# Local attention of a two-layer transformer block: queries and keys held by token and then transposed

## What is computed

```python
h = shift_token(x)
q, k, v = jnp.split(h @ wqkv, 3, axis=-1)       # 8 heads of 64
q = l2norm(q) * qs
k = l2norm(k) * ksc
q, k = rotary_xpos(q, k)                        # q*cos*scale + rotate_half(q)*sin*scale
o = local_attention(q, k, v)                    # windows of 64 tokens, each looks at itself and the one before
x = x + o @ wo
```

## Time and profile before

| | |
|---|---|
| median of 3 runs | 2448.23 us (2447.64 to 2449.12) |
| span of the profiled execution | 2427.7 us, 65264 instructions |
| PE busy | 2292.7 us (94%) |
| DVE busy | 1861.0 us (77%) |
| ACT busy | 1802.1 us (74%) |
| POOL busy | 1477.1 us (61%) |

### The profile page before, as it was taken

One profiled execution on the slowest core, in us unless ns is written; L12 is line 12 of the kernel. 1 busy time (PEld: TensorE's weight loads), 2 busy tenths in 40 slices (PEclk: granted clock), 3 DMA queues, 4 the chain that ended last, 5 costly groups with the idle time before them and its releaser, 6 DMA issues. The chain is left out here.

```text
span 2427.7 us, 65264 instructions
## 1 busy us (share of the span) xinstructions
PE 2292.7 (94%) x21510; PEld 1689.7 (70%) x21510; DVE 1861.0 (77%) x4164; ACT 1802.1 (74%) x5994; POOL 1477.1 (61%) x1402
## 2 busy tenths in 40 slices
PE   5898999996898999999999999888999999999999
PEld 3894666663895888845888854774888864888863
DVE  4784888874786999955999964775999964999974
ACT  3455888883447999955999964337999973999982
POOL 5672777774674777733777740432787851878760
PEclk8897999998999999999999999999999999999999
DMA  6111000001112000000000000000000000000000
GB/s 243 45 45 38 2 0 0 0 1 41 45 45 98 7 6 9 4 5 3 8 8 6 6 1 1 1 1 7 8 6 9 6 1 5 11 6 6 9 1 35
DMA packets 34263, 47.49 MB, mean 20 GB/s; under 512 B 6384, under 2 KB 27760, under 8 KB 33744
## 3 DMA queue, kind: packets, MB, share of 16 engines
q1 hardware_dynamic: 29584, 36.45, 4.8%
q0 software_dynamic: 4544, 9.35, 1.2%
HBM read 24.44 MB, written 12.96 MB: 15 GB/s over the span
## 5 line engine op out<-in xcount | busy, mean ns | idle before, releaser
L265 POOL TENSOR_TENSOR space<-space,tabs 128x512 f32<-128x512 f32 x256 | 326.0, 1273 | 286.4 <-DVE space L369 270.0
L289 ACT ACTIVATE space<-psum,space 128x128 f32<-128x128 f32 x1024 | 357.6, 359 | 4.9 <-DVE space L373 4.9
L262 POOL TENSOR_TENSOR space<-space 128x512 f32<-128x512 f32 x256 | 266.2, 1040 | 149.2 <-DVE space L357 149.2
L269 POOL TENSOR_TENSOR space<-space 128x512 f32<-128x512 f32 x256 | 324.8, 1269 | 26.8 <-POOL space L265 7.6
L173 PE MATMUL psum<-space,big 128*128 128x256 f32 x1024 | 264.4, 381 | 10.4 <-DVE space L369 7.2
L1006 POOL TENSOR_TENSOR space<-space 128x256 f32<-128x256 f32 (+1 forms) x256 | 221.1, 884 | 85.5 <-DVE space L1107 83.4
L353 DVE CAST psum<-cb 128x512 f32<-128x512 bf16 x256 | 177.8, 694 | 87.8 <-ACT space L289 87.8
L1051 ACT ACTIVATE space<-psum,space 128x128 f32<-128x128 f32 (+1 forms) x512 | 209.7, 441 | 1.7 <-DVE space L1100 1.7
L196 PE MATMUL psum<-space,cf 128*128 128x384 f32 x512 | 208.6, 489 | 0.0
L289 ACT ACTIVATION_READ_ACCUMULATOR space<-psum,space 128x1 f32 x1024 | 205.3, 200 | 0.0
L173 PEld LDWEIGHTS psum<-space,big 128*128 128x128 f32 x1024 | 175.1, 191 | 29.9 <-issue 16.7
(11 more groups left out here) (193 smaller groups left out, 5636.1 us busy)
## 6 DMA issues: line engine op xcount, KB each, us to landing
big<-early SPq DMA_DIRECT2D x1, 6688.0 KB
space<-sorted_x SPq DMA_DIRECT2D x78, 64.5 KB, 1.9
z<-token_y SPq DMA_DIRECT2D x16, 256.0 KB, 5.6
space<-z SPq DMA_DIRECT2D x64, 64.0 KB, 1.9
space<-z SPq DMA_DIRECT2D x64, 63.8 KB, 2.0
big<-late SPq DMA_DIRECT2D x1, 3114.0 KB, 13.7
x<-x_t SPq DMA_DIRECT2D x4, 512.0 KB, 6.6
x_final<-x SPq DMA_DIRECT2D x8, 256.0 KB, 2.0
```

Source lines behind the costliest of these rows:

```text
L262: pool.tensor_tensor(x, x, rl[:, (j - 3) % 2, :, :].rearrange("p h t -> p (h t)").unsqueeze(2).to_broadcast([P, 4, P]), ALU.mult).then_inc ...
L265: pool.tensor_tensor(tS[:, :], t2[:, :], tab[:, 1, :], ALU.mult).then_inc(ts_ready, 1)
L269: pool.tensor_tensor(t3[:, j % 2, :], t1[:, j % 2, :], tS[:, :], ALU.add).then_inc(summed, 1)
L289: ins = act.activation(pr[:, (j - 3) % 2, h, t * P:(t + 1) * P], s_ps[h][:, t * P:(t + 1) * P], ACT.Exp, bias=nm[:, (j - 3) % 2, h, t:t + ...
```

## The change

Queries and keys are now projected with tokens on the partitions: the activations are the stationary operand and the weights are streamed (L176 of the changed kernel). With the channels along the free axis, the norm is a DVE reduction to eight numbers for each token (L365), Ln and Exp work on 128x8 (L311, L315), and the half swap is a read of PSUM in another order inside a DVE multiplication (L382), so that the shuffle and POOL's sine multiplication go. POOL adds (as before) and multiplies by 1/norm broadcast over 64 channels. PE then transposes the finished queries and keys (four 128x128 transpositions, L254), and ACT copies them to SBUF (L294). The `head64` matmuls go.

The values are held once, not twice: the product of probabilities and values is done in tiles of 64 rows x 64 columns (L208), the two row halves into banks 2 and 6; ACT copies the one half (L321) and DVE adds the other to it (L390). The transposed probabilities go into one bank and are copied by ACT alone (L300). The projection of values moves from unit s-1 to unit s and stands behind the transposition of probabilities; the exponentials move from unit s-3 to s-2 and stand late in ACT's step. The row sums are written into PSUM. The residual addition stands ahead of the row maximum. The table products move from DVE (behind the first routing) to POOL (ahead of the small-head stage).

```diff
+    qk_ps, qkT_ps, pt_ps, z_ps = g.bank[0], g.bank[1], g.bank[5], g.bank[7][:, 0:T]
+    v_ps, ol = g.bank[2][:, 0:T], (g.bank[2][:, T:2 * T], g.bank[6][:, 0:T])
+    s_ps, s_pair, ls = (g.bank[3], g.bank[4]), g.bank_pair3[:, :, 0:T], g.bank_pair3[:, :, T:T + 2]
...
+                    pe.wait_ge(rotated, S0 + s)
+                for t in range(2):
+                    ins = mm(qk_ps[:, t * T:(t + 1) * T].rearrange("p (n c) -> p n c", n=2), hT[:, k, t * P:(t + 1) * P], wq[:, 0:2, j, :],
+                             start=(t == 0), stop=(t == 1), skip_group_check=True)
                 ins.then_inc(proj_ready, 1)
...
-                mm(ss_ps[:, 0:3 * P], g.head64[:, :], sq[:, (j - 1) % 2, 0:3 * P], start=True, stop=True, skip_group_check=True)
...
-                mm(ss_ps[:, 3 * P:], g.head64[:, :], sq[:, (j - 1) % 2, 3 * P:], start=True, stop=True, skip_group_check=True).then_inc(ss_ready, 1)
...
+                pe.wait_ge(qk_ready, S0 + u + 1)
+                pe.wait_ge(masked, S0 + u + 1)
+                for w, q0, spans in ((0, 0, ((0, 0, WIN),)), (1, LD, ((0, 0, P),)), (0, P, ((P, P, WIN), (P + WIN, WIN, WIN))), (1, P + LD, ((P, P, P),))):
...
+                pe.wait_ge(pt_ready, S0 + u + 1)
...
+                if is_first(u):
+                    prev.free(pe, 6)
+                for spans in (((0, P, 0), (0, P + WIN, 0)), ((P, P, 1), (P + WIN, WIN, 1))):
+                    for r, (q0, n, tile) in enumerate(spans):
+                        rows = slice(r * WIN, (r + 1) * WIN)
+                        for h in range(2):
+                            ins = mm(ol[r][h * LD:(h + 1) * LD, q0:q0 + n], v[rows, j, tile, h * LD:(h + 1) * LD], pt[rows, j % 2, h, q0:q0 + n],
+                                     start=(q0 == 0), stop=True, skip_group_check=True)
...
+                        ins = nc.tensor.transpose(pt_ps[:, h * T + t * P:h * T + (t + 1) * P], pr[:, (j - 3) % 2, h, t * P:(t + 1) * P], g.ident32)
+                ins.then_inc(ptp_ready, 1)
...
+            if runs(s, U):
+                if is_first(s):
+                    prev.free(pe, 2)
+                if at_least(s, 1):
+                    pe.wait_ge(v_ready, S0 + s)
+                if at_least(s, 4):
+                    pe.wait_ge(o0_ready, S0 + s - 3)
+                for t in range(2):
+                    ins = mm(v_ps[:, t * P:(t + 1) * P], hT[:, k, t * P:(t + 1) * P], wq[:, 2, j, :], start=(t == 0), stop=(t == 1), skip_group_check=True)
+                ins.then_inc(vp_ready, 1)
+
+            u = s - 1
+            if runs(u, U):
+                pe.wait_ge(scaled, S0 + u + 1)
+                if is_first(u):
+                    prev.free(pe, 1)
+                if at_least(u, 1):
+                    pe.wait_ge(qk_ready, S0 + u)
+                for n in range(2):
+                    for t in range(2):
+                        ins = nc.tensor.transpose(qkT_ps[:, n * T + t * P:n * T + (t + 1) * P], t3[:, (j - 1) % 2, t * T + n * P:t * T + (n + 1) * P], g.ident32)
+                ins.then_inc(turned, 1)
...
+                u = s - 1
+                if runs(u, U):
+                    pool.wait_ge(rn_ready, S0 + u + 1)
+                    pool.wait_ge(summed, S0 + u + 1)
+                    x = t3[:, (j - 1) % 2, :].rearrange("p (m d) -> p m d", m=8)
+                    pool.tensor_tensor(x, x, rn[:, (j - 1) % 2, :].unsqueeze(2).to_broadcast([P, 8, LD]), ALU.mult).then_inc(scaled, 1)
...
-                    pool.tensor_tensor(tS[:, :], t2[:, :], tab[:, 1, :], ALU.mult).then_inc(ts_ready, 1)
...
+                    pool.wait_ge(rotated, S0 + s + 1)
...
+                        pool.wait_ge(turned, S0 + s - 1)
+                    pool.tensor_tensor(t3[:, j % 2, :], t1[:, j % 2, :], t2[:, j % 2, :], ALU.add).then_inc(summed, 1)
...
+            u = s - 2
+            if only is None and runs(u, U):
+                act.wait_ge(turned, S0 + u + 1)
+                if at_least(u, 2):
+                    act.wait_ge(s_ready, S0 + u - 1)
+                act.activation(qk[:, j % 2, :], qkT_ps, ACT.Copy).then_inc(qk_ready, 1)
...
+            u = s - 4
+            if only is None and runs(u, U):
+                act.wait_ge(ptp_ready, S0 + u + 1)
+                if at_least(u, 2):
+                    act.wait_ge(ol_ready, S0 + u - 1)
+                act.activation(pt[:, j % 2, :, :].rearrange("p h n -> p (h n)"), pt_ps, ACT.Copy).then_inc(pt_ready, 1)
+            if begins(s, only):
+                act.wait_ge(proj_ready, S0 + s + 1)
+                if at_least(s, 2):
+                    act.wait_ge(ss_ready, S0 + s - 1)
+                act.activation(sq[:, j % 2, :], qk_ps, ACT.Square).then_inc(sq_ready, 1)
...
+            u = s - 1
+            if runs(u, U):
+                act.wait_ge(ss_ready, S0 + u + 1)
+                act.activation(lnn[:, (j - 1) % 2, :], ss[:, (j - 1) % 2, :], ACT.Ln, scale=float(2 ** 20), bias=g.tiny[:, 0:1]).then_inc(ln_ready, 1)
+                act.wait_ge(ln_ready, S0 + u + 1)
+                if at_least(u, 2):
+                    act.wait_ge(scaled, S0 + u - 1)
+                act.activation(rn[:, (j - 1) % 2, :], lnn[:, (j - 1) % 2, :], ACT.Exp, scale=-0.5, bias=g.tiny[:, 1:2]).then_inc(rn_ready, 1)
+            u = s - 4
+            if runs(u, U):
+                act.wait_ge(ol_ready, S0 + u + 1)
+                if at_least(u, 2):
+                    act.wait_ge(o_ready, S0 + u - 1)
+                act.activation(o0[:, j % 2, :], ol[0], ACT.Copy).then_inc(o0_ready, 1)
+            u = s - 2
             if runs(u, U):
                 act.wait_ge(nm_ready, S0 + u + 1)
                 if at_least(u, 2):
-                    act.wait_ge(pt_ready, S0 + u - 1)
+                    act.wait_ge(ptp_ready, S0 + u - 1)
...
+                        ins = act.activation(pr[:, j % 2, h, t * P:(t + 1) * P], s_ps[h][:, t * P:(t + 1) * P], ACT.Exp,
+                                             bias=nm[:, j % 2, h, t:t + 1], accum_out=ls[:, h, t:t + 1])
...
-                act.activation(lnn[:, :], ss_ps[:, :], ACT.Ln, scale=float(2 ** 20), bias=g.tiny[:, 0:1]).then_inc(ln_ready, 1)
...
-                act.activation(ss_ps[:, :], lnn[:, :], ACT.Exp, scale=-0.5, bias=g.tiny[:, 1:2]).then_inc(rn_ready, 1)
+                act.wait_ge(vp_ready, S0 + s + 1)
+                if at_least(s, 4):
+                    act.wait_ge(ol_ready, S0 + s - 3)
+                act.activation(v[:, j, :, :].rearrange("p a b -> p (a b)"), v_ps, ACT.Copy).then_inc(v_ready, 1)
...
+            u = s - 3
+            if only is None and runs(u, U):
+                dve.wait_ge(p_ready, S0 + u + 1)
+                if at_least(u, 2):
+                    dve.wait_ge(normed, S0 + u - 1)
+                dve.reciprocal(rl[:, (j - 3) % 2, :, :], ls).then_inc(rl_ready, 1)
...
-                dve.scalar_tensor_tensor(qk[:, j % 2, :], ss_ps[:, :], 1e12, t3[:, j % 2, :], ALU.min, ALU.mult).then_inc(qk_ready, 1)
...
+            if only is None and runs(u, U):
+                if is_first(u):
                     prev.free(dve, 3)
                     prev.free(dve, 4)
-                dve.tensor_copy(g.bank_pair3[:, :, 0:BAND], band).then_inc(masked, 1)
...
+                dve.tensor_copy(s_pair, band).then_inc(masked, 1)
+            u = s - 1
+            if only is None and runs(u, U):
+                dve.wait_ge(sq_ready, S0 + u + 1)
                 if at_least(u, 2):
-                    dve.wait_ge(normed, S0 + u - 1)
-                dve.reciprocal(rl[:, (j - 3) % 2, :, :], ls[:, (j - 3) % 2, :, :]).then_inc(rl_ready, 1)
-            if j == 1 and runs(b - 2, B):
+                    dve.wait_ge(ln_ready, S0 + u - 1)
+                dve.tensor_reduce(ss[:, (j - 1) % 2, :], sq[:, (j - 1) % 2, :].rearrange("p (m d) -> p m d", m=8), AX.X, ALU.add).then_inc(ss_ready, 1)
...
+            u = s - 2
+            if only is None and runs(u, U):
+                dve.wait_ge(s_ready, S0 + u + 1)
+                dve.tensor_reduce(nm[:, j % 2, :, :], s_pair.rearrange("p h (t n) -> p h t n", t=2), AX.X, ALU.max, negate=True).then_inc(nm_ready, 1)
+            if begins(s, only):
+                if is_first(s):
+                    dve.wait_ge(g.tabled, 8)
+                dve.wait_ge(sq_ready, S0 + s + 1)
...
-                dve.stream_shuffle(t2[:, :], qk_ps[:, :], [lane ^ 16 for lane in range(32)]).then_inc(shuffled, 1)
...
+                dve.tensor_tensor(t1[:, j % 2, :], qk_ps, tab[:, 0, :], ALU.mult)
+                halves = lambda x: x.rearrange("p (m a e) -> p m a e", m=8, a=2)
+                dve.tensor_tensor(halves(t2[:, j % 2, :]), halves(qk_ps)[:, :, ::-1, :], halves(tab[:, 1, :]), ALU.mult).then_inc(rotated, 1)
...
+                dve.wait_ge(o0_ready, S0 + u + 1)
...
-                dve.tensor_copy(oT[:, j % 2, :], ol).then_inc(o_ready, 1)
+                dve.tensor_tensor(oT[:, j % 2, :], ol[1], o0[:, j % 2, :], ALU.add).then_inc(o_ready, 1)
...
```

(34 more changed lines are left out.)

166 lines of the change are left out of this document (34 added, 132 removed).

## The result

The changed kernel took 2336.10 us (median of 4 runs, 2334.01 to 2340.24), the kernel before 2448.68 us (4 runs, 2447.64 to 2449.48): a ratio of 0.9538 with a 95% interval of 0.9526 to 0.9550.

The account below looks back on a forecast made before the run. ACT was taken to bound the kernel; a step would fall from 4.505 to 4.20 us, 78 us over 4 x 64 units, less 6 for the stages' ends: 2448.2 - 72 = 2376 us, 8-in-10 range 2345 to 2430.

Parts of the forecast that it names:

- the ring that was forecast to set the step: Local-attention step: ACT's copies, PE's scores and product, ACT's copy of its half, then exponentials, 4.20 us together.
- ACT is the bound, and PE has next to nothing in hand: Step of the kernel before: ACT sets the pace at 4.49 us, PE at most 0.1 below by its own work.
- The exponentials, 1.54: ACT's four exponentials in a step: 1.54 us, kept unchanged in ACT's sum and in the expected ring.
- ACT's own sum: All of ACT's work in a step of the changed kernel: 4.01 us, down by 0.48.
- I leave them at 0.65: PE's scores in a step: left at 0.65 us, though two of ten matmuls lose 64 columns.
- POOL's scaling is in the ring: Rival: ACT, POOL's scaling and PE's transpositions set the step at 4.23 to 4.28 us; 2396 us in all; chance 0.14.
- The sign that I had set for being wrong: In a steady window, a wait ahead of ACT's first copy for PE's last transpositions would point to POOL's ring.
- ACT alone binds: Rival: the wait for PE is short, the product quick, and ACT's 4.01 to 4.1 us rule; 2339 us; chance 0.12.
- The sum: Whole kernel: 0.305 us less a step over four stages of 64 units, 78 us, less 6, gives 72 us.
- The 6 us for the stages' ends: Filling and draining of the four stages: a charge of 1.5 us a stage, 6 in all.
- That offset stays: Whole kernel: the median of runs stood 20.5 us above the profile's span of 2427.7 and would still do so.
- the rival that went with it: PE's clock falls through gaps and more transpositions; slower kernel, 2471 us at one step in ten; chance 0.05.

Follow-up runs that it names:

- before_light_act: The kernel before without ACT's two copies for the third arrangement of the values: 2425.42 us, ratio 0.9983.
- before_sums_psum: The kernel before with the exponentials' row sums in PSUM and the reciprocal ahead of the mask copy: 2447.14 us, ratio 0.9995.
- before_light_wo: The kernel before with PE's output projection over half its columns in three steps of four: 2408.92 us, ratio 0.9921.
- ln_before_square: The changed kernel with ACT's Ln and Exp of the norm moved ahead of the square: 2339.09 us, ratio 0.9629 to the kernel before.
- wo_between: The changed kernel with PE's output projection moved between the scores and the product: 2466.27 us, ratio 1.0152 to the kernel before.
- before_light_pe: The kernel before without two of its ten scores matmuls, the scores of one block of 64 queries: 2429.45 us, ratio 1.0000.
- sums_sbuf: The changed kernel with the exponentials' row sums written to SBUF in place of PSUM: 2332.78 us, ratio 0.9526 to the kernel before.
- split_scale: The changed kernel with POOL's scaling in two halves, each followed by its two transpositions: 2301.47 us, ratio 0.9476 to the kernel before.

## Why the prediction was wrong

In one sentence: the ring that was forecast to set the step, over ACT's exponentials at 4.20, is 3.67 with the measured terms, and the step is set by the ring over POOL's scaling, 3.96 to 4.04, which the forecast had laid aside.

**Which engine bound.** "ACT is the bound, and PE has next to nothing in hand" failed. Both sums were 4.49, and the tie was broken by the list of waits. But 0.16 of ACT's 1.54 was a wait for the projection, too short to be listed: the projection begins at 1792.69 and lasts 1.03, to 1793.72, and the square begins at 1793.75, the 0.03 of a hand-over later. Those two rows stood in the forecast's own groups. The waits in the earlier trace rows (DVE for ACT, PE's weight load for DVE) did not hold PE up either: the weight load was idle while PE's matmuls ran back to back. before_light_act, before_sums_psum and before_light_wo show it.

**The exponentials, 1.54.** They took 1.20 in the changed kernel: 0.16 was the wait, 0.18 the row sums, which are quicker into PSUM. This entered ACT's sum and the ring. ACT's own sum after is 0.30 + 0.49 + 0.48 + 0.48 + 0.33 + 0.21 + 0.27 + 1.20 = 3.76, not 4.01 (the 0.30 of the values' copy and the 0.33 of Ln from ln_before_square, where nothing held them up). Ln and Exp cost 0.33 + 0.21 = 0.54 against 0.45.

**The scores, "I leave them at 0.65".** They took 0.43. wo_between puts 0.16 of the 0.22 down to what follows: scores and product now have the same tiles, 64x64, and with 128x128 behind them the scores need 0.59. The other 0.06 may be the 64 columns fewer in two matmuls, but this was not tried alone, and before_light_pe, where two whole matmuls fewer saved nothing, speaks against it: it stays open.

**The ring that I expected.** It exists, and its path was right, but with the measured terms it is 0.30 + 0.76 + 0.43 + 0.71 + 0.27 + 1.20 = 3.67 over ACT's copy (3.78 over DVE's mask), in place of 4.20: 0.34 and 0.22 of the difference are the two terms above. So it does not bind.

**The rival that did.** "POOL's scaling is in the ring" named the path, and with 1.04 for the scaling gave 4.0; it was laid aside since 4.0 lay below 4.20. It is 4.04 in the step shown and 3.96 in most. I had priced it, as the case that decides, with 1.27, though the nearest row was the 1.04. The sign that I had set for being wrong, ACT's first copy waiting for PE's last transpositions, came in. The rival "ACT alone binds" gave 2339, 3 us from what was measured, by luck: it took ACT's sum for 4.01 to 4.1, which is 3.76, and sums_sbuf put 0.18 on ACT at no cost.

**The sum.** The mean step fell by 0.44, not 0.305: on 252 steps that is 112 us in place of 77. The 6 us for the stages' ends did not show: the stretches from first to last projection account for 112 of the 112.6 us. 35 + 6 are about the 40 us by which I missed. "That offset stays" did no harm, but its reason was wrong.

**What held.** The product's interval (0.61, forecast 0.59), the projection's weights as moving operand (record of 1.03 as before; the scores come 0.96 after its start, behind the end of ACT's first copy, where 0.86 was forecast), the transpositions at 0.44, the table products hidden, the loads at nothing, and the clock: 1.00 in all steady windows with eight transpositions a step. The Trainium skill (TensorE: Matmul & The Clock Gate, Part 4: PE-mode transpose) says that transpositions do not count as PE activity for the clock as matmuls do. The steady windows do not bear out the rival that went with it; the clock fell only for some 3 us while each of two stages filled.

## What to carry to other kernels

When two engines' sums tie to within the shortest wait that the profile lists, each sum of starts can hold unlisted waits: compare the start of each suspect with the end of what it needs, and take 0.5 off each engine in turn before believing either. Work out every ring with its likeliest price and let the longest bind; once one is cut, the next one that had been "safely below" is the forecast. In an order of instructions written by hand, moving one piece forward to shorten a ring can close another one behind it, so name what it is then waiting for.

## What the runs showed of the hardware

- The four exponentials with row sums start 0.30 apart when the sums go to PSUM and 0.345 apart when they go to SBUF, in both kernels (1.20 and 1.38 for four).
- The scores on 64x64 tiles took 0.43 us for 20 matmul records when more 64x64 tiles followed, 0.59 when 128x128 did, 0.65 ahead of 128x64 ones (0.70 in every fourth step of the kernel before); leaving out 4 of the 20 records ahead of 128x64 ones saved nothing.
- Scaling 128x512 with a broadcast operand took POOL 1.04 us in one instruction and 1.18 in two; half of it took 0.61.
- The same program took 2428 to 2429 us on two chips and 2450 on another with equal steps, at a granted clock of 1.00 in them; in the two executions recorded the difference lay ahead of the first of the four stages (18 us).
- In split_scale the turn of PE's loop of eight steps left PE's weight load idle for 0.56 us, in the changed kernel for 0.35.
